# An audio-tower layer on one core: choosing both opening chunks' stacked words on TensorE, scores ahead of transposes and quadratic forms, row sums turned once a chunk, output stored by token

## What is computed

```python
h = tok(x)                                    # B=4, T=750, D=128
h = h + attn(layernorm(h))                    # 4 heads of 32
h = h + ffn(layernorm(h))                     # over the feature axis, 128x128
# tok: x_diff[t] = x[t]-x[t-1]; x_emb = x_diff W_ve' + b_ve
#      h = (ewma forward + ewma backward)/2 @ W_lin' + b_lin,  alpha 0.1
# attn: q, k = l2norm(x wq), l2norm(x wk); v = x (basis v_coeffs')
#      scores[q,k] = q.k * decay**(k-q-1) for k > q only; out = scores v @ o_w' * out_scale
# ffn: (gelu(x tril(W1)' + b1)) tril(W2)' + b2
```

## Time and profile before

| | us |
|---|---|
| median of 3 runs | 84.94 (84.73 to 85.48) |
| profiled execution, its own time | 85.14 |
| its span, first to last instruction | 83.4 |
| TensorE matmuls busy | 72.2 (87%) |
| VectorE busy | 58.3 (70%) |
| ScalarE busy | 39.9 (48%) |
| GpSimd busy | 36.2 (43%) |

### The profile page before, as it was taken

How to read it: one execution, slowest core, us unless ns; L and a number is a source line. 1 busy time by engine, 2 the same in 40 slices (tenths; PEclk the granted TensorE clock), 3 DMA queues, 4 the chain that set the end, 5 groups by cost and what they waited for, 6 DMA issues and landing times.

```text
span 83.4 us, 2740 instructions
## 1 busy us (share of the span) xinstructions
PE 72.2 (87%) x1070; PEld 57.1 (69%) x1070; DVE 58.3 (70%) x176; ACT 39.9 (48%) x93; POOL 36.2 (43%) x51
## 2 busy tenths in 40 slices
PE   2996899999468967998999999999999997978830
PEld 2992786794108976886767986798679975835820
DVE  4798359989593068992997489938993599693340
ACT  0523449943472073063666266636664625584410
POOL 5896408350839200069511923192409100667700
PEclk9999999999999985899999999999999999999999
DMA  0852000221245240000000040003000310004054
GB/s 10 216 141 78 0 0 15 34 43 23 50 93 110 51 92 0 8 0 0 8 0 4 0 108 23 0 8 98 25 8 4 82 52 0 0 0 123 0 127 119
DMA packets 7781, 3.66 MB, mean 44 GB/s; under 512 B 3473, under 2 KB 7753, under 8 KB 7769
## 3 DMA queue, kind: packets, MB, share of 16 engines
q1 hardware_dynamic: 7013, 3.20, 16.3%
q10 hardware_dynamic: 628, 0.22, 1.1%
q0 software_dynamic: 128, 0.07, 0.8%
HBM read 0.99 MB, written 1.54 MB: 30 GB/s over the span
## 4 chain that ended last, share of the span: by engine, by line
PE 64%; ACT 9%; SPq 9%; DVE 6%; issue 4%; DMA 3%; POOL 1%; DVEq 0%; POOLq 0%
SPq L237 9%; PE a_ps L1016 8%; PE s_ps L962 7%; PE s_ps L1049 6%; PE s_ps L808 6%; PE s_ps L1066 5%; PE r_ps L990 5%; PE r_ps L977 5%; PE r_ps L883 3%; DMA z_stk<-z_lo 3%; PE r_ps L1037 3%; DVE prob L662 2%; PE k_ps L920 2%; PE a_ps L941 2%; PE s_ps L906 2%
## 5 line engine op out<-in xcount | busy, mean ns | idle before, releaser
L662 DVE TENSOR_TENSOR prob<-s_ps,dmask 125x500 f32<-125x500 f32 x24 | 14.9, 672 | 0.7 <-PE s_ps L962 0.4
L346 POOL TENSOR_TENSOR h_b<-h,b_row 125x512 f32<-125x512 f32 (+1 forms) x7 | 7.8, 1124 | 12.5 <-DVE h L726 10.4
L324 POOL TENSOR_TENSOR q_dec<-qT,powers 128x500 f32<-128x500 f32 x5 | 5.8, 1161 | 10.3 <-ACT qT L420 10.3
L450 ACT ACTIVATE xn<-h,rstd 125x128 f32<-125x128 f32 x20 | 6.4, 390 | 6.2 <-POOL rstd L336 6.2
L726 DVE SCALAR_TENSOR_TENSOR h<-a_ps,rec,h_tok 125x128 f32<-125x128 f32 x22 | 6.2, 344 | 2.2 <-PE a_ps L1016 2.2
L1016 PE MATMUL a_ps<-o_T,rT 128*125 128x128 f32 x44 | 6.9, 305 | 0.9 <-ACT rT L440 0.9
L962 PEld LDWEIGHTS s_ps<-qT,kT 32*125 32x125 f32 x192 | 5.9, 183 | 2.7 <-issue 2.5
L962 PE MATMUL s_ps<-qT,kT 32*125 32x125 f32 x192 | 6.9, 279 | 0.9 <-ACT gram_z L482 0.9
L990 PE MATMUL r_ps<-prob,v_sc 125*32 125x125 f32 x192 | 6.6, 277 | 1.2 <-DVE ss L635 0.7
L1016 PEld LDWEIGHTS a_ps<-o_T,rT 128*125 128x125 f32 x44 | 6.2, 213 | 1.6 <-ACT rT L440 1.4
L712 DVE TENSOR_TENSOR y<-s_ps,h_b 125x512 f32<-125x512 f32 (+1 forms) x6 | 3.9, 647 | 4.8 <-PE s_ps L1066 4.8
(11 more groups left out here) (181 smaller groups left out, 155.4 us busy)
## 6 DMA issues: line engine op xcount, KB each, us to landing
out_dram<-y SPq DMA_DIRECT2D x5, 224.0 KB
z_stk<-z_hi SPq DMA_DIRECT2D x8, 62.5 KB, 2.1
z_stk<-z_lo SPq DMA_DIRECT2D x4, 62.5 KB, 2.7
out_dram<-y SPq DMA_DIRECT2D x2, 112.0 KB
xt<-in_x_dram SPq DMA_DIRECT2D x1, 188.0 KB, 2.8
out_dram<-y SPq DMA_DIRECT2D x5, 26.0 KB
w<-in_L_ffn_W_dram SPq DMA_DIRECT2D x2, 64.0 KB, 2.1
z_stk<-z_hi SPq DMA_DIRECT2D x8, 15.6 KB, 2.3
```

The costliest lines, as they stand in the source:

```text
L346: pool.tensor_tensor(h2_b[n][:, b0:b1, :], h2[n][:, b0:b1, :], b2_row[:, :].unsqueeze(1).broadcast_to([C, b1 - b0, D]), ALU.add)\
L450: act.activation(xn[n][:, b, :], h2[n][:, b, :], ACT.Copy, scale=rstd2[n][:, b:b + 1])\
L662: dve.tensor_tensor(prob[i % 2][:, h, :, :], sc_ps[h][0:C, 0:W4].rearrange("p (b t) -> p b t", b=B), dmask[:, h, :].unsqueeze(1).broadcast ...
```

## The change

- Opening: the 10 unread matmuls become 7, and 3 behind the product with `w_lin`. ScalarE copies `ve_raw` ahead of `lin_T`. GpSimd's fill of ones is cut in two (500 columns before the difference `xd`, 2000 behind it). z of chunk 4 is added on VectorE.
- `select(1)`: chunk 4's words, too, come through `pick` on TensorE (bank `k0_ps`), ScalarE and VectorE; SyncE's 12 transfers for chunk 4 are gone, those for chunks 0 to 3 stay.
- `project_qk(0)` and `scores(0)` stand ahead of quads and transposes; the late quads stand between the weights' products; VectorE's order follows (two probs ahead of powers and quads).
- `forms`: the three constants come from weights of 32 columns, not 125.
- `sums`: the ones (32 columns, each of the three forms in its own 32 output rows) are the weights and `quad` the moving operand, 250 or 500 columns; VectorE adds the constants and the floor in one operation on 96 rows; then a transpose for each chunk (`turn_sums`) and the square root from PSUM. `sums(1)` moves from ahead of `retrieve(0)` to behind `recall(1)`, `project_kv(1)` ahead of `attention_out(0)`, `project_h(1)` behind `retrieve(1)`.
- ScalarE takes `r_out(0)` ahead of `roots(1)` and the gelu table, and `h_out(1)` behind `r_out(1)`.
- The output in DRAM is laid out token in chunk, chunk, batch, feature, so one partition's 4 batches are 2048 contiguous bytes (512 before); the host puts the axes in order afterwards.

```diff
-WARM = 10
+WARM = (7, 3)
+GR = 96
...
+        SLOT = [2, 0, 1]
...
+        def turned_sums(group):
+            return r_ps[0:C, 2 * D:2 * D + 2 * GR] if group == 0 else s0_ps[0:C, 0:4 * GR]
...
-            for group, (c0, c1, landed) in enumerate(((NC - 2, NC - 1, zstk1_d), (0, NC - 2, zstk_d))):
-                sp.wait_ge(zhi_ok, group + 1)
-                stack(0, z_hi, c0, c1, landed)
-                stack(2, z_hi, c0, c1, landed)
-                sp.wait_ge(zlo_ok, group + 1)
-                stack(1, z_lo, c0, c1, landed)
+            for part, src in ((0, z_hi), (2, z_hi), (1, z_lo)):
...
-                    sp.dma_start(out[:, c * C + r0:c * C + r1, :].rearrange("b t f -> t b f"),
+                    sp.dma_start(out[r0:r1, c, :, :],
...
-            pool.memset(z_stk[3 * CH:STK, 0:LAST, :, :].bitcast(F32), 1.0).then_inc(zone_ok, 1)
+            pool.memset(z_stk[3 * CH:STK, LAST - 1, :, :].bitcast(F32), 1.0).then_inc(zone_ok, 1)
...
+            pool.memset(z_stk[3 * CH:STK, 0:LAST - 1, :, :].bitcast(F32), 1.0).then_inc(zone_ok, 1)
...
+            def select_high(j):
+
+                act.wait_ge(sel_s, j + 1)
+                act.activation(flat(z_stk[0:3 * CH, LAST - j, :, :]), (s3_ps, k0_ps)[j][0:3 * CH, 0:W4], ACT.Copy)\
+                    .then_inc(selhi_ok, 1)
...
+            late_gram(0)
             act.wait_ge(mix_ps, 1)
...
-            late_gram(0)
             late_gram(1)
+            late_gram(2)
             roots(0)
...
             h_out(0)
+            r_out(0)
             roots(1)
             act.activation(table_in[:, :], xd[:, 0:1], ACT.Gelu).then_inc(table_ok, 1)
-            r_out(0)
-            h_out(1)
             q_out(2)
             k_out(2)
             r_out(1)
+            h_out(1)
...
+                dve.tensor_scalar(ss_row[:, t0:t1], (r_ps, s0_ps)[group][0:GR, 0:t1 - t0], gram_c[:, 0:1],
+                                  floor_c[:, 0:1], ALU.add, ALU.max).then_inc(ss_ok, 1)
...
+            probs(1, 0)
+            carry_on(0)
+            for h in range(1, H):
+                probs(1, h)
+            values(1)
             sums(1)
...
             residual(0)
-            values(1)
             keys(1)
             statistics(0)
+            scales(1)
             carry_on(1)
...
+                    pe.wait_ge(late_ok, 3)
+                    pe.wait_ge(prob_ok, H + 1)
                 for a in range(3):
...
+                    ins = pe.matmul((r_ps, s0_ps)[group][SLOT[a] * CH:(SLOT[a] + 1) * CH, 0:t1 - t0],
+                                    ones_blk[:, min(a, 1), :], quad[:, a, t0:t1], start=True, stop=True)
                 ins.then_inc(ss_ps, 1)
 
+            def turn_sums(group):
+
+                c0, c1 = GROUPS[group]
+                pe.wait_ge(ss_ok, group + 1)
+                for c in range(c0, c1):
+                    ins = pe.transpose(turned_sums(group)[:, (c - c0) * GR:(c - c0 + 1) * GR],
+                                       ss_row[:, c * C:(c + 1) * C], ident[0:GR, 0:GR])
+                ins.then_inc(sst_ps, 1)
...
+                if i == 2:
+                    pe.wait_ge(root_ok, 2)
```

More of the change, by code:

```diff
@@ L760, in _ @@
             probs(0, 1)
-            sums(0)
+            low_words(a_ps[:, 0:D], H0, H0 + D, 2)
+            dve.tensor_tensor_scan(powers[:, :], dec_col[:, 2:3].broadcast_to([D, C + 1]), first_one[:, :],
+                                   0.0, ALU.mult, ALU.add).then_inc(pow_ok, 1)
+            for a in range(3):
+                quads(a)
             decay(2)
             probs(0, 2)
+            sums(0)
             decay(3)
             probs(0, 3)
+            dve.wait_ge(w21_ok, 1)
+            low_words(k0_ps[:, 3 * D:4 * D], V0, H0, 3)
             scales(0)
@@ L806, in _, with unread @@
             pe.wait_ge(ident_ok, 1)
-            for _ in range(WARM):
-                pe.matmul(s3_ps[:, 0:D], ident, ident, start=True, stop=True)
+            def unread(n):
+                for _ in range(n):
+                    pe.matmul(s3_ps[:, 0:D], ident, ident, start=True, stop=True)
+            unread(WARM[0])
             pe.wait_ge(lin_in, 16)
@@ L1068, in ffn_2 @@
                 ins.then_inc(f2_s, 1)
-            select()
+            select(0)
+            select(1)
             pe.wait_ge(qkT_ok, 1)
             forms()
-            pe.matmul(s1_ps[0:STK, 0:D], VE[:, :], lin_T[:, 0:D], start=True, stop=False)
-            pe.matmul(s1_ps[0:STK, 0:D], BL[:, :], ident, start=False, stop=True).then_inc(hrep_ps, 1)
+            project_qk(0)
+            pe.matmul(a_ps[0:STK, 0:D], VE[:, :], lin_T[:, 0:D], start=True, stop=False)
+            pe.matmul(a_ps[0:STK, 0:D], BL[:, :], ident, start=False, stop=True).then_inc(hrep_ps, 1)
             pe.wait_ge(bas_in, 16)
-            pe.matmul(s0_ps[:, 0:STK], w_basis[:, :], proj_T[:, 0, :], start=True, stop=True)\
+            pe.matmul(a_ps[:, D:D + STK], w_basis[:, :], proj_T[:, 0, :], start=True, stop=True)\
                 .then_inc(bct_ps, 1)
-            project_qk(0)
+            scores(0)
+            for piece in range(3):
+                quads(piece)
             pe.wait_ge(vo_in, 32)
             pe.wait_ge(tril_ok, 2)
+            pe.wait_ge(sello_ok, 2)
             for j, w in enumerate((w_vc, w_oc, w_basis, w_1)):
```

233 lines of the change are left out of this document (107 added, 126 removed).

## The result

The change makes the kernel slower: 88.60 us (median of 4 runs, 87.74 to 88.72) for 84.84 (4 runs, 84.70 to 85.48), a ratio of 1.041 [1.032, 1.049]. Forecast were 82.1 us, in a range of 80.8 to 84.0. A second comparison gave the same, 88.21 us and 1.041 [1.036, 1.046]. The profiled execution took 88.59 us, 86.8 of them span.

What follows compares the result with a forecast made beforehand. TensorE was taken to bound the kernel, so step 2's start counts: 2.6 us gained up to the output and 0.4 there cut the span from 83.4 to 80.4, plus 1.74 around it gives 82.1 us, range 80.8 to 84.0.

Steps and rivals of the forecast that it cites:

- the first and fourth rivals: Clock rivals; the first: one fall like the old one, 1.3 us, giving 83.4, chance 0.2; the fourth has its own line.
- the fourth rival: Lower clock from the thin stretch (20.9 to 24.8) until step 2: 6 us of cost gives 88, chance 0.07.
- the third rival: GpSimd wins the shared port at decay 3 and its next product runs first: 1.25 us more, 83.4, chance 0.1.
- Decay 3: VectorE operation at 21.3 beside a late GpSimd product: costs nothing, or one more product of 1.25 us.
- Decay 1: VectorE operation at 14.6 beside z_lo, counted as ending at 15.85; its prob is needed at 17.8, so no cost.
- The opening: Start to scores(0): it runs at 13.0, not 15.02, so 2.0 us earlier.
- The run of TensorE to the end of the sums: From scores(0) to the end of sums(0): no gap if nothing is late, 7.9 us, to 20.9.
- The sums: Three matmuls per group, about three side by side: 0.6 us for group 0, 0.9 for group 1, bounds 0.85 and 2.5.
- the second rival: The sums run one after the other: 0.7 and 1.6 us more on the way, 84.4, chance 0.1.
- To retrieve(0): After sums(0), 3.9 us through VectorE's chain to scores(1) at 24.8; retrieve(0) at 25.9, 3.9 us earlier.
- the mark: attention_out(1), 10.0 us behind retrieve(0)'s start: at 35.9 for 38.34 before, a gain of 2.4 us.
- The output: End of the kernel: larger DMA pieces shorten the last transfers by 0.4 us, between 0 and 0.8.

Runs made afterwards that it cites:

- the run with the output's layout: Only the output laid out by token as in the change, in the kernel before: 87.49 us, ratio 1.026.
- the fill: An unread VectorE memset (128 x 1040) between sums(0) and probs(0, 3), added to the changed kernel with decays moved: 86.97 us, ratio 1.026.
- the run with the decays moved: The changed kernel with decay(2) and decay(3) on VectorE ahead of its three quads: 83.39 us, ratio 0.971.
- the pair of runs: The changed kernel with earlier decays and 18 unread matmuls, with the new output layout (83.52 us) and the old one (83.80 us).
- the first place filled: The changed kernel with 3 unread matmuls behind sums(0) and 7 ahead of project_kv(0), none ahead of attention_out(1): 84.44 us, ratio 0.994.
- its repetition: The changed kernel unchanged, measured again beside the kernel before on another chip: 88.21 us, ratio 1.041.

## Why the prediction was wrong

**The clock, given 0.07 where it rises to the cost that decides.** The step that failed is the argument against the first and fourth rivals: "21.62 to 25.26 was as thin before (1.70 of 3.64) and stayed at 1.00". That the clock falls behind the thin stretch, from 24.9 on, is the fourth rival's sign and its cause. Its course was another: the rival had one low stretch that holds until step 2, and there were two, with the clock at 1.00 from 31.7 to 41.8 between them. And its time (88 forecast, 88.60 measured) came out by luck: it put the clock at 6 us, which cost 3.8 by the two profiles (2.37 and 1.39). The rest of the 6.5 us above the forecast of 82.1 is the third rival's decay with its wait (1.37), the slower opening of that execution (0.77) and 0.6 that the forecast's other terms had too small. The stretch before was a bad witness in two ways. It was broken by transfers and late quads, while the new one has 0.54 us of work in 3.08; and that it stayed at 1.00 was no sign of room, as the run with the output's layout shows: the same instructions with a low clock from 27.1 for 10.4 us. The clock's cost was put too high for the rival (6 us; 3.8 by the decays' move, 3.7 to 4.0 by the unread matmuls) and its chance too low: a change that makes the stretch ahead of a fall thinner had to be given more than 7 in 100. "One idle gap brought one low stretch of 3.3 us, no more" was an argument from a single case.
The Trainium skill (TensorE: Matmul & The Clock Gate, What's actually happening) states that an idle stretch brings the lower clock. The runs with the fill and with unread matmuls agree: 1 us more of waiting and the clock goes to 0.50; work of no use in the wait and it stays at 1.00. The row of before bore it out less than the prediction says: ahead of the old fall TensorE stood idle for 0.7 us (29.14 to 29.83), and the clock fell only at 30.6, in the middle of `retrieve(0)`.

**Decay 3, counted as nothing.** "Decay 3 waits for a product ending about when the sum is done: nothing again, or one more product of 1.25" took the first end. Measured, it was 1.35 us for 0.41, so 0.94: near the other end, and named the third rival, with 0.1. The cause is in the rows of GpSimd: the three products have no gap between them (3.81 us for 3), the third begins at 21.78, and VectorE's scan comes at 22.02, 0.24 us too late, and ends 0.27 behind it. In the four other profiles with this order it comes as late behind the third product (0.24 or 0.25 us) and takes 1.35 or 1.36. So the forecast had the right rule and did not follow it to its end: by its own numbers (first `gram_z` at 18.7, 1.25 a product) the second product ends at 21.2, and the decay, due at 21.3, meets the third. All of it came 0.6 to 0.7 us later, in that order. Whether a scan that stands ready when one product ends gets in ahead of the next, no run shows. Decay 1 cost nothing, as forecast: it took 1.25 us beside z_lo and ended at 16.41, and prob 1, behind it, at 17.13, ahead of the late quad at 18.36.

**The two belong together.** The rivals were treated as separate, each with its price. But the third makes the stretch longer and so sets off the fourth: 0.94 us on VectorE cost some 5 us in all (88.60 with it, 83.39 without; 5.1 between the two profiles behind the opening). Without it the stretch is close to what the forecast counted: 1.75 us of TensorE work in the 3.90 behind the sums, for 1.6 in 3.9. There the clock did stay at 1.00 in the profile, and gave way somewhere in two of the four executions; so the argument from the old stretch was weak for the stretch that was forecast, and wrong for the one that came. A chance for the clock should have been given for each length of the thin stretch.

**The opening.** `scores(0)` started at 13.36 (13.0 forecast), and at 12.58 in the profile of the run with the decays moved, whose opening is the same program. The 2.0 us were 1.7 in the one profile and 2.4 in the other. The three unread matmuls behind L824 took 1.49 us (6 records) in the one and 0.83 in the other, with the granted clock at 1.00 in both; that explains most of the 0.78 between them; why they took longer is open. In the faster openings TensorE is no longer what is last: with 18 unread matmuls the chain there runs over VectorE, whose z ends at 8.18 and lets `select` begin at 8.32.

**The run of TensorE to the end of the sums.** Forecast 7.9 us; 8.18 and 8.19 in the two profiles. Right.

**The sums.** 0.59 and 1.00 us for 0.6 and 0.9. The bounds were 0.85 and 2.5; the three groups of 32 rows do run side by side, and the second rival falls. By the Trainium skill's 2.38 (TensorE: Matmul & The Clock Gate, Measured speedup vs the span model) the estimate was 1.05 for group 1. Measured against the 2.5 us of six records in a row it is 2.5 / 1.00 = 2.5.

**To retrieve(0).** 3.9 us from the end of the sums to `scores(1)`, of which 0.4 were the decay: 5.73 after (1.84 of it issue, and 0.51 more than without the fall from `project_kv(0)` to `scores(1)`), 3.85 with the decay away. That last is 0.35 more than the 3.5 which the forecast's terms leave.

**From retrieve(0) to the mark.** 10.0 us forecast; 11.65 after and 10.69 at full clock. The terms that were small: VectorE's operation on 500 columns (0.81 for 0.65) and the four transposes (0.69 for 0.5). So at full clock the mark would have come at 36.46 for 35.9. Of the forecast's 3.0 us of span, the 0.4 of the output included, the run with the decays moved gives 2.5 (83.4 - 80.9).

**The output.** 0.28 us by the pair of runs, 0.20 to 0.28 by the time between the last y and the end (2.71 before, 2.43 to 2.51 with the new layout); forecast 0.4, between 0 and 0.8.

**What stays open.** When the clock falls and how long it stays low is shown by these runs only as far as the pairs go: a fall ended after 3.3 to 3.4 us, 6.7 to 6.9 or 10.4, and the same instructions gave 3.3 and 10.4. Why a second fall needs the first was not found. Whether the old opening would have stood the new order was not tried.

## What to carry to other kernels

Where the trace shows one fall of the granted clock, the next order may have more of it, as here: before anything is reordered there, add up TensorE's work in the stretches ahead, and count a wait that grows by 1 us at several times its length (3.6 to 3.8 us here). Where VectorE has an operation with two operands in SBUF and GpSimd a train of products, put the operation ahead of the train, even if that is long before it is needed; here that one move was worth 5 us, most of them the clock's. An unread matmul in a stretch that TensorE waits through anyway is the test for both the cause and the cure: if the kernel gets faster with more work in it, it was the clock.

## What the runs showed of the hardware that was not expected

- In these profiles the clock falls once or twice, and the second fall comes only behind a first: idle for 1.9 us ahead of the mark, TensorE kept its clock in two kernels (with the decays moved, and with the first place filled) and lost it in three (after, its repetition, with the delay of 0.93 us on VectorE), all of which had lost it before.
- The same instructions up to 48 us had the clock low from 30.75 to 34.10 in one profile and from 27.1 to 37.5 in another (mark 38.34 and 40.81).
- VectorE's scan, begun 0.24 us behind the start of a product of GpSimd, ends 0.27 behind its end: 1.35 us for 0.41.
- Six records of unread matmuls in the opening took 0.83 us in one profile and 1.49 in another, both at a granted clock of 1.00.
